# The end of a two-layer decoder on one core: the last two groups' steps written out, gathers issued first, and a routing count moved ahead

## The chip, the cores and the metric

The kernel runs on one core of a Trainium2 chip. The metric is the device time of one execution in microseconds, the median of several runs. TensorE (PE in the rows), VectorE (DVE), ScalarE (ACT) and GpSimd (POOL) each take their instructions in order from a queue of their own; SyncE (SP) issues transfers. They wait for each other through semaphores.

## What is computed

Eight sequences of 256 rows of 256 numbers pass through two decoder layers, all in float32. Layer 0 is causal self attention with 16 heads, cross attention to 120 context rows, and a mixture of eight experts of which each row takes two. Layer 1 is a gated self attention with an MLP, a cross attention with four heads and a mix of each row with the row before it. After each of the six parts the input is added and the row normalised:

```python
def _L1_xattn_ref(query_data, key_data, value_data, Wq, Wk, Wv, Wp, bp):
    q = split_heads(query_data, Wq); k = split_heads(key_data, Wk); v = split_heads(value_data, Wv)
    scores = jnp.einsum('bhqd,bhkd->bhqk', q, k) / np.sqrt(DK) + causal
    return jnp.einsum('bhqk,bhkd->bhqd', softmax(scores), v).transpose(0, 2, 1, 3).reshape(B, S, D_MODEL) @ Wp.T + bp

def _L1_ffn_ref(x, W_r, W_k, W_v, mu_r, mu_k):
    x_prev = jnp.concatenate([jnp.zeros((B, 1, C)), x[:, :-1, :]], axis=1)
    xr, xk = mu_r * x + (1.0 - mu_r) * x_prev, mu_k * x + (1.0 - mu_k) * x_prev
    r = jax.nn.sigmoid(xr @ W_r.T)
    return r * (jnp.square(jax.nn.relu(xk @ W_k.T)) @ W_v.T)

x = _layernorm(x + _L0_attn_ref(x, ...));  x = _layernorm(x + _L0_xattn_ref(x, ctx, ...))
x = _layernorm(x + _L0_ffn_ref(x, ...))
x = _layernorm(x + _L1_attn_ref(x, ...));  x = _layernorm(x + _L1_xattn_ref(x, ctx, ctx, ...))
x = _layernorm(x + _L1_ffn_ref(x, ...))
```

Inside `_L1_attn_ref` the attention's output is added to the row, normalised, and goes through the MLP: up to 1024 numbers, GELU, down to 256.

## The kernel before, in words

Three stages follow each other: `attention_layers`, `expert_layer` and `last_layers`. The 2048 rows are in four groups of two sequences, so a group is 512 rows or four tiles of 128. Nothing is scheduled by a tool: each stage has a block of instructions per engine, written in the order in which the engine runs them, and every wait is a `wait_ge` on a semaphore. An instruction behind a wait waits too, whatever it needs itself. The PSUM memory into which PE writes is eight banks; a product that reuses a bank waits until its reader is done.

**attention_layers.** At its end the routing of rows to experts is made up. DVE chooses two experts for each row (`choose`, its last lines L614 to L620), PE counts them (`count`, L461 to L465), and from the counts DVE works out each row's place (`rank`, from L628). One-hot tables in four batches of eight (made by POOL at L312 and L314, the last batch's second half by DVE at L759) are multiplied on PE (`place`, L473) into a table of sources. In PE's order for the last group all eight products of the third batch stand ahead of `count`. POOL and DVE both raise the semaphore `hothigh`.

**expert_layer.** Rows are handled in 39 tiles of 128, sorted by expert. For tile j POOL gathers the rows with an indirect DMA (`gather`, L810), PE turns them (`turn_rows`, L832), ACT copies them (L880), PE multiplies with the up weights (`up`, L846), ACT has copied the expert's up weights to a fixed place for that (`copy_weights`, L895) and takes the sigmoid (L884), POOL multiplies gate and sigmoid (L819), DVE finishes the hidden rows (L935 to L944), PE multiplies down (L857), DVE adds the bias (`result`, L951) and ACT issues the store (L910). ACT's order for a tile is: wait for the result of tile j, store it, copy the weights of tile j + 2, sigmoid of tile j + 1, copy the rows of tile j + 2. PE's order is: up of j + 1, turn j + 2, down of j. POOL issues the gather of tile j + 2 after the multiplication for tile j. SP has loaded three experts (1.5 MB each, with a bias) ahead of the stage and loads the next when one is found ready (`load_expert`, L156 to L160); at the start of the stage it issues the next three at once.

**last_layers.** The groups go through a pipeline of three steps: `a`, the self attention; `r`, its output product (`wout`), the MLP up (L1194 through `up`, eight products of 512 columns) and down (L1314, four tiles), then the context keys and values; `z`, the cross attention and the mix. A period works on `a` of one group, `r` of the one before and `z` of the one before that. Of the six periods (`PERIODS = G + 2`) the last two have no `a`: period 4 has `r` of group 3 (the last) and `z` of group 2, period 5 has only `z` of group 3. They run the same loop body with the parts for `a` left out.

The parts of `z` on which the change bears, in their order: queries (`wxq`), scores of the first sequence (`context_scores`, L1273), DVE's maximum (`context_max`, L1844 to L1849), 16 exponentials and sums on ACT (`context_exp`, L1556), DVE's scaling (`context_scale`, L1858), turning of the probabilities (`context_turn`, L1283) through one bank and ACT's copy (L1563), the same for the second sequence, sums (`context_sums`, L1294) and ACT's copies (L1607), the output product (`context_product`), the normalisation (L1796 to L1806 and L1790 on DVE, `rstd` on POOL), turning (L1203), ACT's copy (L1724), POOL's difference with the row before (L1172), DVE's mix (`mix`, L1814), products with `wk2` and `wr`, ACT's relu and tanh (L1733, L1736), DVE's square (L1987), and for each of four tiles a product with `wv2` and DVE's `mix_result` (L1898, L1900) through one bank.

## Time and profile before

| | |
|---|---|
| median of 3 runs | 1390.38 us (1387.86 to 1391.41) |
| the profiled execution's own time | 1385.69 us |
| its span | 1384.0 us |
| PE, DVE, ACT, POOL busy | 1141.3, 737.2, 575.2, 415.1 us |
| mean granted clock of TensorE | 0.934 |

The profiled execution's time is the span with 1.7 us around it. PE is busy for most of the span; its matrix instructions are pipelined and their ends modelled, so that busy is not the same as at full speed. The granted clock is 1.00 or 0.50: 2.4 or 1.2 GHz. `attention_layers` ends near 525 us, `expert_layer` near 776 us, and periods 4 and 5 of `last_layers` take the stretch from 1229.8 us on. A row of a timeline begins with its start and duration in microseconds; in brackets stands how long its engine had been idle and what ended that. One float32 product of two matrices (a `product` of `KD` = 2 parts) shows as four MATMUL records.

### The profile page before, as it was taken

Reading aid. Unit: us, or ns where it says so; the run is one execution under the profiler, and the core shown is the slowest. Engines: PE = TensorE matmul, PEld = TensorE weight load, DVE = VectorE, ACT = ScalarE, POOL = GpSimd, SP = SyncE. Lnnn points to the kernel's source line nnn. Section 1 sums busy time; section 2 is a strip of 40 time slices with the busy share of each in tenths; the row PEclk is TensorE's granted clock in tenths of the full one; section 3 lists DMA queues with packets and bytes.
Section 4 is the critical chain, followed back from the end, with each engine's and each line's share of the span. In section 5 each row is a group of like instructions: output and inputs, shape, how many; then the busy total and the mean of one; then the engine's idle time right before and its main releaser. Section 6 shows DMA issues by size and latency. Waiting matters only on the chain. (4 is left out here: it accounts for less than half of the span.)

```text
span 1384.0 us, 19896 instructions
## 1 busy us (share of the span) xinstructions
PE 1141.3 (82%) x6666; PEld 784.5 (57%) x6666; DVE 737.2 (53%) x2208; ACT 575.2 (42%) x1386; POOL 415.1 (30%) x508
## 2 busy tenths in 40 slices
PE   7889979988997865999999363877988998997965
PEld 3456456445645654988989332544645654664643
DVE  1563484367248443555555337484495868563334
ACT  1461272246117212444444052544665465434241
POOL 0250052025005673444444424033224222220111
PEclk9999999999999977999999776998999998997967
DMA  5000100020010407111111331001001000000000
GB/s 181 16 2 0 52 16 1 8 60 2 1 52 1 150 16 266 40 47 47 42 44 47 108 129 31 1 0 32 8 1 31 1 23 0 1 24 0 1 16 15
DMA packets 40223, 52.34 MB, mean 38 GB/s; under 512 B 10780, under 2 KB 33372, under 8 KB 40124
## 3 DMA queue, kind: packets, MB, share of 16 engines
q1 hardware_dynamic: 31100, 36.66, 8.2%
q0 software_dynamic: 3408, 9.31, 2.3%
q10 hardware_dynamic: 5616, 5.11, 1.1%
q8 instruction: 54, 0.88, 0.3%
q14 instruction: 45, 0.37, 0.1%
HBM read 41.76 MB, written 9.31 MB: 37 GB/s over the span
## 5 line engine op out<-in xcount | busy, mean ns | idle before, releaser
L1194 PE MATMUL bank<-words 128*128 128x512 f32 (+3 forms) x736 | 266.1, 512 | 36.3 <-ACT words L1547 17.3
L1194 PEld LDWEIGHTS bank<-words 128*128 128x128 f32 (+1 forms) x736 | 140.8, 199 | 137.4 <-issue 77.2
L357 PE MATMUL bank<-words 128*128 128x512 f32 x384 | 172.5, 601 | 8.3 <-DMA words<-in_wq 8.3
L323 POOL TENSOR_TENSOR words<-words 128x256 f32<-128x256 f32 (+1 forms) x128 | 103.5, 829 | 189.9 <-DVE words L694 189.9
L846 PEld LDWEIGHTS bank<-words 128*128 128x128 f32 x1248 | 146.9, 194 | 5.6 <-ACT words L880 3.7
L846 PE MATMUL bank<-words 128*128 128x128 f32 x1248 | 147.4, 277 | 3.1 <-ACT words L880 3.1
L565 ACT ACTIVATE words<-words 128x128 f32<-128x128 f32 (+1 forms) x256 | 113.3, 444 | 50.0 <-DVE words L689 50.0
L895 ACT ACTIVATE words<-words 128x2048 f32 x39 | 74.5, 1911 | 133.5 <-issue 133.5
L357 PEld LDWEIGHTS bank<-words 128*128 128x128 f32 x384 | 72.5, 193 | 90.1 <-issue 89.5
L547 ACT ACTIVATE words<-bank 128x512 f32<-128x512 f32 x48 | 28.7, 597 | 192.0 <-PE bank L357 192.0
L819 POOL TENSOR_TENSOR words<-words 128x512 f32<-128x512 f32 x39 | 49.4, 1268 | 136.3 <-ACT words L884 136.3
L604 DVE COPY words<-bank 128x512 f32<-128x512 f32 x48 | 33.2, 691 | 105.7 <-PE bank L357 105.4
L685 DVE CUSTOM_DVE_ANT_0 words<-bank,words 128x128 f32<-128x128 f32 (+1 forms) x256 | 76.0, 353 | 20.6 <-PE bank L368 18.7
L857 PE MATMUL bank<-words 128*128 x312 | 75.5, 385 | 0.7 <-DVE words L944 0.7
L128 POOL TENSOR_TENSOR words<-words 128x4 f32<-128x4 f32 x12 | 2.4, 200 | 243.5 <-DVE words L110 167.3
L1135 POOL TENSOR_TENSOR words<-words 128x2 f32<-128x2 f32 x32 | 6.9, 216 | 216.1 <-DVE words L1806 216.0
L935 DVE TENSOR_SCALAR words<-bank,words 128x128 f32<-128x128 f32 x156 | 44.1, 345 | 51.3 <-PE bank L846 51.1
L381 PE MATMUL bank<-words 128*128 128x128 f32 x384 | 55.1, 280 | 18.6 <-DVE words L700 10.5
L368 PE MATMUL bank<-words 64*128 64x128 f32 (+1 forms) x512 | 58.2, 348 | 8.6 <-DVE words L689 5.2
L394 PE MATMUL bank<-words 128*64 128x256 f32 (+1 forms) x512 | 55.8, 337 | 10.4 <-ACT words L573 9.4
L700 DVE COPY words<-bank 128x768 f32<-128x768 f32 x64 | 59.7, 932 | 8.3 <-PE bank L381 8.3
L381 PEld LDWEIGHTS bank<-words 128*128 128x128 f32 x384 | 41.0, 141 | 39.5 <-issue 31.8
(233 smaller groups left out, 2021.3 us busy)
## 6 DMA issues: line engine op xcount, KB each, us to landing
words<-in_w SPq DMA_DIRECT2D x8, 1024.0 KB, 10.3
y_slots<-words ACTq DMA_DIRECT2D x39, 128.0 KB, 1.7
words<-in_w SPq DMA_DIRECT2D x8, 512.0 KB, 10.9
words<-in_xt SPq DMA_DIRECT2D x4, 512.0 KB, 3.8
words<-in_x SPq DMA_DIRECT2D x4, 512.0 KB, 4.3
x_rows<-words SPq DMA_DIRECT2D x16, 128.0 KB, 1.8
words<-in_wm SPq DMA_DIRECT2D x2, 1024.0 KB, 6.8
out_x<-words SPq DMA_DIRECT2D x16, 128.0 KB, 1.8
```

The costliest lines, as they stand in the source:

```text
L323: last = pool.tensor_tensor(part, part, inv[:, j % SLOTS0, :, t:t + 1].to_broadcast([P, 2, P * (t + 1)]), ALU.mult)
L357: last = pe.matmul(bank[c % 2][:, :], w, r, start=k == 0, stop=k == KD - 1)
L368: last = pe.matmul(bank[SCORES[i % 2][n]][:, t * P:t * P + P * (t + 1)],  kt[r, m, b * S + t * P:b * S + (t + 1) * P], qt[r, m, b * S:b * ...
L381: last = pe.transpose(bank[2 + n][:, k * P:(k + 1) * P], prob[:, j % SLOTS0, n, c:c + P], ident[:, :])
L394: last = pe.matmul(bank[4 + j % 2][DH0 * n:DH0 * n + DH0, queries], v[:, 2 * b + k, h * DH0:(h + 1) * DH0], probt[:, j % 2, n, probs_of], ...
L565: last = act.activation(prob[:, i % SLOTS0, n, c], prob[:, i % SLOTS0, n, c], ACT.Exp, bias=negmax[:, i % SLOTS0, n, t:t + 1], scale=DH0 * ...
L685: dve.tensor_tensor_reduce(out=prob[:, i % SLOTS0, n, c], in0=bank[SCORES[i % 2][n]][:, c], in1=mask0[:, c], scale=1.0, scalar=-3e38, op0= ...
L700: dve.tensor_copy(probt[:, j % 2, :, :], turned).then_inc(tcopied, 1)
L846: last = pe.matmul(bank[(BANKG, BANKV)[half][j % 2]][:, c * P:(c + 1) * P], wfix[:, j % 2, k * 2 * FF + half * FF + c * P:k * 2 * FF + hal ...
L857: last = pe.matmul(bank[BANKY[j % 2]][:, 0:D], hidden[:, j % 2, k * P:(k + 1) * P], w2[:, bass.ds(e * W2 + k * D, D)], start=k == 0, stop= ...
L895: act.activation(wfix[:, j % 2, :], w1[:, bass.ds(e * W1, W1)], ACT.Copy).then_inc(wcopied, 1)
L1194: last = pe.matmul(out, w, r, start=i == 0, stop=i == len(pairs) - 1)
```

## The change

It has three parts. In `attention_layers` PE makes four of the eight products of the third one-hot batch ahead of `count` and four behind it; DVE's half of the last batch raises a semaphore of its own. In `expert_layer` POOL issues the gather of tile j + 2 ahead of the multiplication for tile j, and SP waits for the first two gathers before it loads the fourth expert. In `last_layers` periods 4 and 5 are no longer run by the loop (`PERIODS = G`); their instructions are written out on each engine. Products and elementwise work are the same in number of rows and columns; what differs is their order, the banks and how they are cut.

```diff
-            def place(first):
-                for n in range(first, first + OH):
+            def place(first, number=OH):
+                for n in range(first, first + number):
                     pe.wait_ge(hotlow, n + 1)
...
                         tail_gate(g)
                         if g == G - 1:
-                            place(2 * OH)
+                            place(2 * OH, OH // 2)
                     if c == COUNT:
                         count(g)
+                        if g == G - 1:
+                            place(2 * OH + OH // 2, OH // 2)
...
                 sp.sem_inc(ready, 1)
+                if e == 0:
+                    sp.wait_ge(gathered[0], 16)
+                    sp.wait_ge(gathered[1], 16)
                 if e + EARLY < NE:
                     load_expert(sp, dram, keep, e + EARLY)
...
             for j in range(SLOT_TILES):
-                pool.wait_ge(gated, j + 1)
-                pool.tensor_tensor(sig[:, :], gate[:, :], sig[:, :], ALU.mult).then_inc(mixed, 1)
                 if j + 2 < SLOT_TILES:
                     pool.wait_ge(rturned, j + 1)
                     gather(j + 2)
+                pool.wait_ge(gated, j + 1)
+                pool.tensor_tensor(sig[:, :], gate[:, :], sig[:, :], ALU.mult).then_inc(mixed, 1)
...
-        PERIODS = G + 2
+        PERIODS, LAST, OTHER = G, G - 1, G - 2
...
+            def last_up(b, i):
+                if b == 1:
+                    pe.wait_ge(m1gelu, i + 1)
+                for c in (2 * i, 2 * i + 1):
+                    last = product(bank[M1BANK[i]][:, batch(c % 2)], [(wm1[:, k, tok(c)], h5t[:, k, batch(b)]) for k in range(KD)])
+                last.then_inc(m1pair, 1)
...
+            context_scores(OTHER, 0)
+            turn(LAST, n5, 0, lambda t: h5[:, t, :], bank[2])
+            pe.wait_ge(n5.copied, 2 * LAST + 1)
+            last_up(0, 0)
+            last_up(0, 1)
+            context_scores(OTHER, 1)
...
+            for c in range(KD):
+                product(bank[2 * c][:, :], [(wk2[:, k, tok(c)], xk[:, k, :]) for k in range(KD)]).then_inc(kmm, 1)
...
+            context_scores(LAST, 0)
+            last_down(3)
...
+            last_queries(1, 1)
...
+            context_scores(LAST, 1, (4, 5))
+            context_turn(LAST, 0, (1, 3), lastsm)
...
+            last_turn(n7, 0, bank[0])
+            last_turn(n7, 1, bank[2])
+            last_mix(0, 6, 7, 1)
+            last_mix(1, 4, 5, 3)
+            last_values(0, 1)
+            last_values(1, 3)
...
+            context_exp(OTHER, 0)
+            mlp_rows(LAST, 0)
+            mlp_rows(LAST, 1)
+            context_exp(OTHER, 1)
+            act.preload_act_table_set("gelu_and_others")
...
+            act.preload_act_table_set("natural_log_exp_and_others")
+            context_exp(LAST, 0, sm=lastsm)
...
+            context_exp(LAST, 1, (4, 5), lastsm)
+            act.preload_act_table_set("gelu_and_others")
+            sums_copy(LAST, 0)
```

How the instructions stand, at the three places of which the prediction speaks. `bank` is the PSUM memory and `words` the SBUF, of which all tiles are parts; a line number is that of the kernel the rows are from.

PE at the end of `attention_layers`, before: the gate (L451), the one-hot products (L473), the count (L461 to L465), the source table (L534).

```order
L451 MATMUL bank<-words 128x8 x8
L473 MATMUL bank<-words 128x128 x8
L461 MATMUL bank<-words 128x32
L462 MATMUL bank<-words 128x32
L465 MATMUL bank<-words 128x8
L473 MATMUL bank<-words 128x128 x8
L534 MATMUL bank<-words 128x39
```

The same place now (products L477, count L462 to L466):

```order
L452 MATMUL bank<-words 128x8 x8
L477 MATMUL bank<-words 128x128 x4
L462 MATMUL bank<-words 128x32
L463 MATMUL bank<-words 128x32
L466 MATMUL bank<-words 128x8
L477 MATMUL bank<-words 128x128 x12
L540 MATMUL bank<-words 128x39
```

Four of the products that stood ahead of the count stand behind it.

PE in period 4 before, from the first scores of group 2 (L1273): turning of group 3's rows (L1203), the second scores, all turning of probabilities (L1283), the sums (L1294) with two up products of 512 columns between.

```order
L1273 MATMUL bank<-words 128x120 x8
L1203 MATMUL bank<-words 128x128 x8
L1273 MATMUL bank<-words 128x120 x8
L1283 MATMUL bank<-words 120x128 x16
L1294 MATMUL bank<-words 64x128 x4
L1194 MATMUL bank<-words 128x512 x2
L1294 MATMUL bank<-words 64x128 x4
L1194 MATMUL bank<-words 128x512 x2
L1294 MATMUL bank<-words 64x128 x8
```

Now (scores L1335, turning of rows L1265, of probabilities L1345, sums L1356, products L1256):

```order
L1335 MATMUL bank<-words 128x120 x8
L1265 MATMUL bank<-words 128x128 x4
L1256 MATMUL bank<-words 128x256 x8
L1335 MATMUL bank<-words 128x120 x8
L1265 MATMUL bank<-words 128x128 x4
L1256 MATMUL bank<-words 128x256 x8
L1345 MATMUL bank<-words 120x128 x8
L1256 MATMUL bank<-words 128x256 x8
L1345 MATMUL bank<-words 120x128 x8
L1256 MATMUL bank<-words 128x256 x8
L1356 MATMUL bank<-words 64x128 x16
```

The whole MLP up, in four pieces of eight matrix multiplications with 256 columns, now stands between the steps of group 2's cross attention.

PE in period 5 before, where group 3 is alone:

```order
L1203 MATMUL bank<-words 128x128 x8
L1194 MATMUL bank<-words 128x512 x4
L1273 MATMUL bank<-words 128x120 x16
L1283 MATMUL bank<-words 120x128 x16
L1294 MATMUL bank<-words 64x128 x16
L1194 MATMUL bank<-words 128x256 x8
L1203 MATMUL bank<-words 128x128 x8
L1194 MATMUL bank<-words 128x512 x4
L1194 MATMUL bank<-words 128x256 x16
```

And now, from the products that precede group 3's first scores:

```order
L1256 MATMUL bank<-words 128x512 x4
L1335 MATMUL bank<-words 128x120 x8
L1256 MATMUL bank<-words 128x256 x16
L1265 MATMUL bank<-words 128x128 x4
L1256 MATMUL bank<-words 128x256 x12
L1335 MATMUL bank<-words 128x120 x8
L1345 MATMUL bank<-words 120x128 x8
L1356 MATMUL bank<-words 64x128 x8
L1345 MATMUL bank<-words 120x128 x8
L1256 MATMUL bank<-words 128x256 x4
L1356 MATMUL bank<-words 64x128 x8
L1256 MATMUL bank<-words 128x256 x4
```

Between group 3's two scores now stand 28 matrix multiplications of 256 columns: the last down tile, group 2's products with `wr` and `wv2`, and group 3's second queries. Behind this the probabilities of the first sequence are turned and summed before those of the second are turned.

## Rows read from the trace of the kernel before

**Rows 1.** Timeline of PE at the end of the routing.
```profile
507.87 2.59 PE L473 MATMUL bank<-words 128*128 128x128 f32 x10
...
514.44 0.47 PE L461 MATMUL bank<-words 128*128 128x32 f32 x2
...
515.15 0.57 PE L465 MATMUL bank<-words 128*128 128x8 f32 x2
```
**Rows 2.** Timeline of DVE at the same place.
```profile
510.55 0.89 DVE L620 TENSOR_TENSOR words<-words 128x8 f32<-128x8 f32 x4
...
515.76 0.28 DVE L628 TENSOR_TENSOR words<-words,bank 128x32 f32<-128x32 f32 x2 [3.65 <-PE bank L465]
```
**Rows 3.** Entry into the experts: first gather, and PE's waits for gathered rows.
```profile
525.87 1.22 POOL L810 DMA_INDIRECT words<-x_rows,words  x1 [3.43 <-POOLq L165]
...
534.27 0.69 PE L832 MATMUL bank<-words 128*128 128x128 f32 x2 [9.66 <-DMA words<-x_rows,words]
...
549.32 0.44 PE L832 MATMUL bank<-words 128*128 128x128 f32 x2 [1.80 <-DMA words<-x_rows,words]
```
**Rows 4.** POOL's instructions between 660 and 700 us, gathers among them.
```profile
DMA to landing us min/median/max: 3.5/3.6/4.1
```
**Rows 5.** POOL's multiplication for the third and the last tile.
```profile
555.80 1.26 POOL L819 TENSOR_TENSOR words<-words 128x512 f32<-128x512 f32 x1 [5.17 <-ACT words L884]
...
771.58 1.26 POOL L819 TENSOR_TENSOR words<-words 128x512 f32<-128x512 f32 x1 [4.89 <-ACT words L884]
```
**Rows 6.** Waits of PE between 560 and 772 us: total, times, longest.
```profile
PE bank L832 <- DMA words<-x_rows,words: 8.3, 19, 1.0
```
**Rows 7.** Timeline of ACT and POOL in one expert tile.
```profile
650.17 1.91 ACT L895 ACTIVATE words<-words 128x2048 f32 x1 [3.21 <-issue]
...
652.68 1.27 POOL L819 TENSOR_TENSOR words<-words 128x512 f32<-128x512 f32 x1 [3.31 <-ACT words L884]
```
**Rows 8.** Windows of PE in periods 4 and 5: us, busy, clock, DMA.
```profile
1245.30:1265.80 20.50, 11.31 (x48) 0.50 0.00 1
...
1327.20:1351.10 23.90, 14.29 (x74) 0.50 0.00 1
...
1358.00:1364.80 6.80, 4.23 (x5) 0.50 0.00 0
...
1229.80:1384.00 154.20, 109.40 (x482) 0.82 0.04 12
```
**Rows 9.** Waits of PE in period 5, from 1317.7 us.
```profile
PE bank L1273 <- ACT words L1556: 5.2, 1, 5.2
PE bank L1194 <- DVE words L1814: 4.1, 1, 4.1
PE bank L1283 <- DVE words L1858: 3.8, 1, 3.8
PE bank L1203 <- DVE words L1790: 2.3, 2, 1.7
PE bank L1194 <- DVE words L1898: 1.6, 3, 0.6
```
**Rows 10.** Period 4: PE's second turning, ACT's copy of group 3's rows, PE's second scores.
```profile
1247.04 1.12 PE L1203 MATMUL bank<-words 128*128 128x128 f32 x4 [2.43 <-DVE words L1790]
...
1249.40 1.97 ACT L1532 ACTIVATE words<-bank,words 128x256 f32<-128x256 f32 x4
...
1249.60 2.07 PE L1273 MATMUL bank<-words 64*128 64x120 f32 x16 [1.44 <-ACT words L1556]
```
**Rows 11.** ACT's change of table in period 4, and the first GELUs.
```profile
1270.41 1.28 ACT L1717 ACT_TABLE_LOAD   x1
1271.70 1.27 ACT L1547 ACTIVATE words<-bank,words 128x512 f32<-128x512 f32 x2
```
**Rows 12.** PE: five products in a stream, and one alone between waits.
```profile
1312.80 4.49 PE L1194 MATMUL bank<-words 128*128 128x256 f32 x20 [0.51 <-DVE words L1898]
...
1372.06 1.13 PE L1194 MATMUL bank<-words 128*128 128x256 f32 x4 [0.59 <-DVE words L1898]
```

More of the change, by code:

```diff
@@ L1474, in _ @@
                     pe.wait_ge(rsig, NT * z + NT)
[L1476 to L1487 removed]
+                if r is None:
                     pe.wait_ge(qkt, NT * a + NT)
@@ L1514, in _, with last_down @@
                     context_values(r)
+            def last_up(b, i):
[4 more added lines that the diff above has]
+                last.then_inc(m1pair, 1)
+            def last_down(t):
+                if t >= 2:
+                    pe.wait_ge(n6.added, NT * LAST + t - 1)
+                product(bank[(3, 1)[t % 2]][:, 0:D], [(m1t[:, k, tok(t)], wm2[:, k, :]) for k in range(MC)]).then_inc(n6.product, 1)
@@ new lines, in last_values @@
+            def last_values(b, out):
+                pe.wait_ge(lastkact, b + 1)
+                for i in range(HALF):
+                    last = product(both(out, b)[:, i, :], [(lastrl[:, k, tok(HALF * b + i)], wv2[:, k, :]) for k in range(KD)])
+                last.then_inc(lastv, 1)
+            pe.wait_ge(utc, QUADS1 * G)
+            turn_heads(LAST, 0)
+            turn_heads(LAST, 1)
+            pe.wait_ge(xvr, GB * OTHER + GB)
+            for b in range(2):
+                turn(OTHER, n6, b, lambda t: x(OTHER, t), bank[6 + b])
@@ new lines, in _ @@
+            turn_output(LAST, 0)
+            turn_heads(LAST, 2)
+            turn_heads(LAST, 3)
+            turn_output(LAST, 1)
+            pe.wait_ge(n6.copied, 2 * OTHER + 2)
+            for c in range(KD):
+                product(bank[6 + c][:, :], [(wxq[:, k, tok(c)], x4t[:, k, :]) for k in range(KD)]).then_inc(xq, 1)
+            for t in range(NT):
+                pe.wait_ge(ogc, 2 * LAST + t // HALF + 1)
+                if t >= 2:
+                    pe.wait_ge(n5.added, NT * LAST + t - 1)
+                else:
+                    pe.wait_ge(ogr, NT * LAST + NT)
+                product(bank[t % 2][:, 0:D], [(ogt[:, k, tok(t)], wout[:, k, :]) for k in range(KD)]).then_inc(n5.product, 1)
@@ new lines, in _ @@
+            context_scores(LAST, 0)
+            last_down(3)
+            pe.wait_ge(mixed, 2 * OTHER + 2)
+            for b in range(2):
+                for i in range(HALF):
+                    last = product(both(4 + b, b)[:, i, :], [(xr[:, k, tok(HALF * b + i)], wr[:, k, :]) for k in range(KD)])
+                last.then_inc(rmm, 1)
+            last_turn(n6, 1, bank[3])
+            pe.wait_ge(kact, KD * OTHER + KD)
+            for t in range(NT):
+                if t >= 2:
+                    pe.wait_ge(n8.added, NT * OTHER + t - 1)
+                product(bank[2 * (t % 2)][:, 0:D], [(rl[:, k, tok(t)], wv2[:, k, :]) for k in range(KD)]).then_inc(n8.product, 1)
@@ L1764, in _, with last_gelu, last_rows @@
                         values_copy(r, b)
+            def last_gelu(b, i):
+                act.wait_ge(m1pair, MC // 2 * b + i + 1)
+                for c in (2 * i, 2 * i + 1):
+                    last = act.activation(m1t[:, c, batch(b)], bank[M1BANK[i]][:, batch(c % 2)], ACT.Gelu, bias=bm1[:, c:c + 1])
+                last.then_inc(m1gelu, 1)
+            def last_rows(b, source):
+                act.wait_ge(n6.turned, 2 * LAST + b + 1)
+                act.activation(half(x4t, b), turned_rows(bank[source]), ACT.Copy).then_inc(n6.copied, 1)
@@ new lines, in _ @@
+            for b in range(2):
+                act.wait_ge(n6.turned, 2 * OTHER + b + 1)
+                act.activation(half(x4t, b), turned_rows(bank[6 + b]), ACT.Copy).then_inc(n6.copied, 1)
+            output_copy(LAST, 0)
+            output_copy(LAST, 1)
+            for c in range(KD):
+                act.wait_ge(xq, KD * OTHER + c + 1)
+                act.activation(qxt[:, c, :], bank[6 + c][:, :], ACT.Copy).then_inc(xqr, 1)
+            context_exp(OTHER, 0)
+            mlp_rows(LAST, 0)
@@ new lines, in _ @@
+            last_queries_copy(0, 5)
+            act.wait_ge(mixed, 2 * OTHER + 2)
+            for c in range(KD):
+                act.wait_ge(kmm, KD * OTHER + c + 1)
+                act.activation(rl[:, c, :], bank[2 * c][:, :], ACT.Relu).then_inc(relu, 1)
+            for b in range(2):
+                act.wait_ge(rmm, NT * OTHER + b + 1)
+                act.activation(rs[:, rows_of(b), :], both(4 + b, b), ACT.Tanh, scale=0.5).then_inc(rsig, 1)
+            act.preload_act_table_set("natural_log_exp_and_others")
@@ new lines, in _ @@
+            mix(OTHER, MUR, xr)
+            add_product(LAST, n6, 2, bank[3])
+            for c in range(KD):
+                dve.wait_ge(relu, KD * OTHER + c + 1)
+                dve.tensor_tensor(rl[:, c, :], bank[2 * c][:, :], rl[:, c, :], ALU.mult).then_inc(kact, 1)
+            add_product(LAST, n6, 3, bank[1])
+            context_max(LAST, 0)
+            normalise(LAST, n6, lambda t: x(LAST, t), 1)
+            dve.wait_ge(rsig, NT * OTHER + 2)
+            for t in range(NT):
+                dve.wait_ge(n8.product, NT * OTHER + t + 1)
+                dve.scalar_tensor_tensor(rs[:, t, :], rs[:, t, :], 1.0, bank[2 * (t % 2)][:, 0:D], ALU.add, ALU.mult).then_inc(n8.added, 1)
+                dve.drain()
+                dve.scalar_tensor_tensor(x(OTHER, t), rs[:, t, :], 0.5, x(OTHER, t), ALU.mult, ALU.add)
```

309 lines of the change are left out of this document (260 added, 49 removed).

## The prediction, made before the changed kernel had run

> **What bounds the kernel now.** I read the page, then the timelines of PE at three places, the waits of PE there, and its windows with the granted clock. PE is busy for 82% of the span (the table above), and where it is not, it stands behind short chains of the other engines. So the edits are worth what they take out of those chains. Three places count.
>
> At the end of the routing PE makes one-hot products until it may count. DVE had chosen the experts at 510.55 + 0.89 = 511.44 us, the count began at 514.44 and ended at 515.72, and DVE went on at 515.76 after 3.65 us of idling for it [rows 1, 2].
>
> At the entry into the experts the first gather is issued at 525.87 and its rows are there at 534.27: 8.4 us, in which PE does nothing [rows 3]. Later gathers take 3.5 to 4.1 us, 3.6 in the middle [rows 4]. The first shares the DMA engines with the three experts of 1.5 MB that SP issues in the same microsecond.
>
> In periods 4 and 5 PE is busy for 109.4 of 154.2 us, at a mean clock of 0.82 [rows 8]. 11.31 + 14.29 + 4.23 = 29.8 us of that is at 1.2 GHz, which at 2.4 GHz would be 14.9. So the stretch is 94.5 us of work at full clock, 14.9 us that the low clock adds, and 44.8 us without work, of which the last 7.4 are DVE's, POOL's and the store's after PE's last product.
>
> **The change part by part.**
>
> *Count moved ahead.* Four products stand ahead of it instead of eight. Five of them took 2.59 us from 507.87 [rows 1], so four end near 509.95, before DVE has chosen at 511.44. The count takes the same 515.72 − 514.44 = 1.28 us and ends at 512.75, and DVE goes on some 2.9 us earlier. What comes behind (DVE's ranks and half one-hot tables, POOL's other half) waits for these ranks and moves with them; POOL is done with its earlier tables before that. The four products behind the count are hidden by DVE's ranking. **2.9 us.** The separate semaphore costs nothing: its only waiter is the same PE product.
>
> *SP waits for the first two gathers.* Gather 0 then runs alone and should land 3.6 us after its issue, at 529.5 instead of 534.27: **4.8 us**. Between 4.1 and 3.5 us of landing it is 4.3 to 4.9; below, nothing, if the 8.4 us is the price of a first gather and not of the sharing. What SP issued at 525.2 it now issues near 531, some 6 us later; the fourth expert is needed after three experts' tiles, at six microseconds a tile, far behind. The Trainium skill, "DMA: Bandwidth & Descriptors", section on queues, rings and completion order, speaks against so much: each DMA engine goes round between the queues that have work, packet by packet. By that rule an estimate would be that sharing at most doubles the 3.6 us, and the wait is worth 3.6 instead of 4.8 us.
>
> *Gathers issued one multiplication earlier.* POOL's own order costs nothing: the issue (some 1.4 us) falls into the 3.3 us in which POOL waits for ACT [rows 7], and starts when it did before. But it is for a tile one later, so each gather has a tile's time more. Three things follow. The third tile's gather no longer stands behind the first multiplication, is issued near 530, and the 1.80 us at 549.32 goes [rows 3]; DVE's result, waiting behind it, comes 2.0 us earlier: **2.0**. In the steady part PE waits 8.3 us for gathers, 19 times [rows 6], but most of this is not on the path: 36 multiplications take 771.58 − 555.80 = 215.8 us, 5.99 each [rows 5], and the loop that sets them is ACT's: copy of weights 1.91, sigmoid 0.6, POOL 1.27 [rows 7], DVE's two instructions 1.1, store and the register read before the next copy 1.0. That is 5.9 us and holds no gather. Its steps stand at 6.03 us for the first 16 tiles and at 5.88 for the later ones, and only single steps exceed these, by 1.5 us together: **1.5**. The last tile has no weights to copy and PE's wait of 1.0 us counts in full: **1.0**. For this part the ends are 0 and 8.3 + 2.0; I stay near the sum 4.5.
>
> *Periods 4 and 5.* The work is the same 94.5 us: a half of 256 columns costs half of 512. What changes is how much stands idle, how often the pipe runs empty, and the clock.
> Idle in period 5 [rows 9]: the 5.2 us for ACT's exponentials goes, because group 2's products with `wr` and `wv2` and group 3's last down tile lie there now. The 1.6 us of the four separate `wv2` results, and the 0.6 before them, go, since they are two products for a half each in banks of their own. The 4.1 and 2.3 us around normalisation and mix (6.4) shrink to about 3.7: one half's chain is covered by the other's products. The 3.8 us for the second scaling stays. Two banks instead of one for turned probabilities take 1.3 of 2.2 us of copies. Sum 11.1 us.
> Idle in period 4: the up products fill the 3.8 us and 2.2 us of the same chain only in part, since each half waits for a GELU or a copy; I count 0.2 saved. One wait is added: the first up product needs ACT's copy of its rows, which stands behind 16 exponentials. The copies begin at 1249.40, half of 1.97 us later PE may start, 1250.4, where the first half's rows are turned at 1247.04 − 2.43 = 1244.6. In place of 2.43 + 1.44 = 3.9 us of waits [rows 10] this is some 5.5: 1.6 lost. Down and `wv2` of different groups no longer follow one another tile by tile, 1.8 saved. Sum 0.4.
> Each wait also lets the pipe run empty: a product alone is 1.13 us, in a stream 4.49 / 5 = 0.90 [rows 12]. Some 15 waits go: 15 × 0.23 = 3.5.
> Clock: it fell at 1245.3 and 1327.2 among waits and came back after steady work. With up products between the scores I expect about 11 us of addition instead of 14.9, as one of the two long stretches stays (the last group's probabilities and scaling). 3.9, with ends of 0 and 10.
> After PE's last product the same chain remains: 0.
> Sum 11.1 + 0.4 + 3.5 + 3.9 = 18.9; laid out with every wait on all four queues at the durations of the trace, 19 to 25 come out, by where the clock falls. I take **20**. The ends are 11 (idle time alone) and 27.
> What ACT's tables cost: the new order has three changes where there were four, but one now lies right before group 3's first exponentials and one behind its second. Load and first GELU follow each other, 1.28 and then 1271.70 [rows 11]; group 2's products cover that. "ScalarE: Activation LUTs", section "What ACT_TABLE_LOAD costs", in the Trainium skill gives about 1.4 us of drain on top; the rows show none. By the page the gain of 20 would be some 2.8 less.
>
> The sum is 2.9 + 4.8 + 4.5 + 20 = 32.2 us. Against the profiled execution's own 1385.69 us this gives 1353.5; that execution was 4.7 us below the median of 1390.38, so on the median's scale it is **1358 us**. A difference of over 0.3%, 4 us, is what a measurement of this kernel can tell.
>
> **The rivals.**
>
> *Half chains bring idle time only.* The clock stays as poor as before, since the interleaved pieces are short and each waits for GELU or copy, and the pipe runs empty as often. Then the end gives 11 to 12: 1390.4 − 2.9 − 9.3 − 11.5 = 1367. For it: the rows at low clock hold work in pieces of one or two microseconds [rows 8]. Against: the new pieces are 3.6 us.
>
> *The first gather is slow by itself.* Nothing is shared away, the 4.8 us stays where it is and with it perhaps half of what follows: 1358 + 4.8 + 2 = 1365. For it: it is the first indirect transfer of the stage. Against: the third, issued under the same loads, was late too.
>
> *The end gains more.* With few waits left the clock stays high through the older group's cross attention: 27 instead of 20, 1351.
>
> *Slower: the clock stays low through periods 4 and 5.* If the cut into halves and the many orders between queues leave PE with a short wait in every piece, so that it is granted 1.2 GHz from 1245 on, all work behind that, some 80 us at full clock, is doubled, and the low clock adds 80 us where the forecast has 11: 1358 + 69 = 1427. It decides for slower from 11 + 32 = 43 us of work at the low clock. The Trainium skill, "TensorE: Matmul & The Clock Gate", has the throttled clock as the default that only activity lifts, which is this mechanism. Against: between 1265.8 and 1327.2 PE kept 2.4 GHz with a dozen short waits.
>
> *The change does not do what it says* hardly applies: its order is to be seen on the queues.
>
> **How the numbers follow.** The forecast has 0.60, the gain at the end without the clock 0.14, the slow first gather 0.10, the better clock 0.12, the slower case 0.03; 0.01 is left for no change. The forecast's own range is 1352 to 1364; with the neighbours and 3 us for where the clock happens to fall in the unchanged middle it is 1348 to 1368. Faster 0.95, same 0.02, slower 0.03.
>
> **What would show it.** Right: DVE's L628 successor starts near 512.9; PE's first turned rows near 526.6 (2.9 earlier and 4.8 less); no PE wait for gathered rows in the steady part and steps of 6.03 and 5.88 us on POOL; between the first `turn_heads` of group 3 and the last normalisation about 132 us instead of 152; PE's wait before the first up product about 5.5 us. Wrong: gathers that still take over 6 us at the entry, tile steps under 5.8 us (then the gather was on the path and the gain is larger), over 20 us of PE work at clock 0.5 in the last 130 us, or a time above 1368.

## The result, and the profile after

The changed kernel takes 1355.14 us (median of 4 runs, 1354.0 to 1355.9) where the kernel before, run beside it, takes 1389.22 us. The ratio is 0.9753, with an interval of 0.9736 to 0.9769. The forecast was 1358 us and faster.

The profiled execution took 1355.9 us, with a span of 1354.0 us. PE is busy for 1137.6 us of it (1141.3 before), at a mean clock of 0.942 (0.934). The two profiled spans differ by 1384.0 − 1354.0 = 30.0 us, the medians by 34.1.

**The count.** Timelines of PE and of DVE at the end of the routing, which answer to [rows 1, 2] (start, duration, engine, line and operation; in brackets the idle time ahead and what ended it):

```profile
507.90 2.05 PE L477 MATMUL bank<-words 128*128 128x128 f32 x8
511.73 0.63 PE L462 MATMUL bank<-words 128*128 128x32 f32 x2 [1.77 <-DVE words L626]
...
512.60 0.57 PE L466 MATMUL bank<-words 128*128 128x8 f32 x2
513.02 2.05 PE L477 MATMUL bank<-words 128*128 128x128 f32 x8
```

```profile
508.08 0.19 DVE L739 COPY words<-bank 128x32 f32<-128x32 f32 x1 [3.89 <-PE bank L452]
...
513.21 0.28 DVE L634 TENSOR_TENSOR words<-words,bank 128x32 f32<-128x32 f32 x2 [0.87 <-PE bank L466]
```

Four products end at 509.95 us, before DVE has chosen, and PE now waits for DVE (1.77 us). DVE's own wait for the count shrinks from 3.65 to 0.87 us, and it goes on at 513.21 instead of 515.76.

**The experts.** POOL's first gathers and the multiplications for the third and the last tile, and PE's first turning of gathered rows; they answer to [rows 3, 5]:

```profile
523.33 1.22 POOL L819 DMA_INDIRECT words<-x_rows,words  x1 [3.43 <-POOLq L165]
...
546.18 1.27 POOL L831 TENSOR_TENSOR words<-words 128x512 f32<-128x512 f32 x1 [3.20 <-ACT words L893]
...
759.32 1.27 POOL L831 TENSOR_TENSOR words<-words 128x512 f32<-128x512 f32 x1 [3.16 <-ACT words L893]
```

```profile
526.46 0.69 PE L841 MATMUL bank<-words 128*128 128x128 f32 x2 [4.39 <-DMA words<-x_rows,words]
```

The rows of the first gather are used 526.46 − 523.33 = 3.13 us after its issue (8.40 before). PE's waits between 550 and 765 us, which answer to [rows 6] (total, times, longest):

```profile
PE bank L855 <- ACT words L889: 4.2, 16, 0.5
PE bank L866 <- DVE words L953: 0.8, 1, 0.8
```

No wait for gathered rows is left, and PE waits for ACT instead. POOL's steps stand at 6.03 and then 5.88 us as before, so the gathers did not set them. That ACT's loop does fits the sum of its durations; no run here changes that loop, so it is not shown. The last step is 759.32 − 754.89 = 4.43 us.

**The end.** Windows of PE in the changed kernel, from the first turning of heads of group 3 on, the stretches at low clock first; they answer to [rows 8] (length; busy time and records; clock; DMA share; GB/s):

```profile
1235.60:1245.90 10.30, 5.18 (x12) 0.50 0.00 0
1256.20:1262.90 6.70, 5.54 (x13) 0.50 0.00 0
1321.00:1324.40 3.40, 3.05 (x12) 0.51 0.00 0
1334.70:1338.10 3.40, 3.40 (x9) 0.52 0.02 5
1220.04:1354.00 133.96, 101.33 (x529) 0.90 0.05 14
```

And its waits there, which answer to [rows 9]:

```profile
PE bank L1256 <- ACT words L1739: 5.9, 1, 5.9
PE bank L1265 <- DVE words L2089: 5.6, 4, 3.2
PE bank L1345 <- DVE words L2157: 3.8, 1, 3.8
PE bank L1345 <- ACT words L1770: 3.5, 2, 2.7
PE bank L1256 <- ACT words L1977: 1.5, 1, 1.5
```

The stretch is 133.96 us instead of 154.14 (1229.86 to the end): 12.2 us less without work (32.6 instead of 44.8) and 8.0 us less of busy time. At low clock lie 5.18 + 5.54 + 3.05 + 3.40 = 17.2 us, which add about 8.6 us (half of it) where it was 14.9. The exponentials' 5.2 us, the waits for single `wv2` results and most of the wait for the mix are gone. The largest wait is now the one that the change added, 5.9 us for ACT's copy of rows; the forecast had 5.5.

### The profile page after: what moved, and what is told of

The parts are those of the page before. It is cut to its first block and busy times, and to the rows that moved or that the text cites. A ratio compares the mean times of both kernels' runs of the same rounds, so it can differ in the third digit from the quotient of the medians.

```text
span 1354.0 us, 20004 instructions
## 1 busy us (share of the span) xinstructions
PE 1137.6 (84%) x6714; PEld 788.5 (58%) x6714; DVE 735.5 (54%) x2208; ACT 574.0 (42%) x1389; POOL 415.8 (31%) x509
## 5 line engine op out<-in xcount | busy, mean ns | idle before, releaser
L1256 PE MATMUL bank<-words 128*128 128x256 f32 (+3 forms) x848 | 282.9, 487 | 37.2 <-ACT words L1754 19.0
L1256 PEld LDWEIGHTS bank<-words 128*128 128x128 f32 (+1 forms) x848 | 165.6, 202 | 130.5 <-issue 70.0
L855 PE MATMUL bank<-words 128*128 128x128 f32 x1248 | 151.7, 281 | 8.4 <-ACT words L889 6.7
L691 DVE CUSTOM_DVE_ANT_0 words<-bank,words 128x128 f32<-128x128 f32 (+1 forms) x256 | 76.0, 353 | 20.6 <-PE bank L369 18.4
L382 PE MATMUL bank<-words 128*128 128x128 f32 x384 | 55.9, 282 | 17.0 <-DVE words L706 9.1
L953 DVE SCALAR_TENSOR_TENSOR words<-words 128x512 f32<-128x512 f32 x39 | 27.0, 694 | 67.3 <-POOL words L831 67.2
```

Source lines behind the costliest of these rows:

```text
L382: last = pe.transpose(bank[2 + n][:, k * P:(k + 1) * P], prob[:, j % SLOTS0, n, c:c + P], ident[:, :])
L691: dve.tensor_tensor_reduce(out=prob[:, i % SLOTS0, n, c], in0=bank[SCORES[i % 2][n]][:, c], in1=mask0[:, c], scale=1.0, scalar=-3e38, op0= ...
L855: last = pe.matmul(bank[(BANKG, BANKV)[half][j % 2]][:, c * P:(c + 1) * P], wfix[:, j % 2, k * 2 * FF + half * FF + c * P:k * 2 * FF + hal ...
L1256: last = pe.matmul(out, w, r, start=i == 0, stop=i == len(pairs) - 1)
```

## The parts one by one

The medians of the kernel before scatter by 12 us on one chip (1382.04 to 1394.34 in 29 runs), and parts of 3 to 5 us drown in that. So I cut each profiled execution at four events that the timelines show: the issue of the first gather, PE's first turning of gathered rows, the end of the last expert product, and the first turning of heads of group 3. In microseconds, each number being the difference of two times of the rows:

| kernel | gather, issue to use | then to the end of the experts | then to the last group's heads | then to the end |
|---|---|---|---|---|
| before | 8.40 | 241.45 | 454.14 | 154.14 |
| changed | 3.13 | 237.00 | 456.58 | 133.96 |
| e1_count | 8.03 | 241.50 | 461.39 | 153.92 |
| e2_loads | 3.10 | 245.32 | 455.99 | 153.89 |
| e3_gather | 8.62 | 236.86 | 456.00 | 153.77 |
| e4_end | 8.27 | 241.16 | 455.36 | 133.55 |
| u1_scores_behind | 2.88 | 238.55 | 456.04 | 137.93 |
| s1_rows | 2.98 | 236.98 | 456.25 | 129.99 |
| s2_warm | 3.03 | 238.57 | 455.16 | 133.94 |
| s3_warm_late | 3.08 | 236.98 | 453.52 | 134.27 |
| s4_warm_start | 3.07 | 236.97 | 453.38 | 133.82 |
| s5_rows_warm | 3.11 | 237.00 | 452.71 | 121.19 |

Where nothing was edited, a stretch repeats within half a microsecond at the end, and twice the experts took 1.6 us more. Between experts and the last heads, which nobody touched but s4 and s5, it varies by 8 us: 453.52 (s3_warm_late) to 461.39 (e1_count). There PE's busy time varies with it, 350.67 us before and 358.38 in e1_count, at mean clocks of 0.90 and 0.87, while the time without work stays at 103.5 and 103.0 us. So in these traces most of the scatter lies there. The time ahead of the first gather is in no column: its issue stands at 525.87 to 528.36 us in the four kernels without the count's edit and at 523.20 to 525.06 in the eight with it.

**The count alone.** In the kernel before:

```diff
-                            place(2 * OH)
+                            place(2 * OH, OH // 2)
...
                         count(g)
+                        if g == G - 1:
+                            place(2 * OH + OH // 2, OH // 2)
```

> The kernel before with the count moved ahead alone. My theory: DVE goes on 2.6 to 2.9 us earlier (the first L634 of the last group near 513.0 us instead of 515.76), everything behind shifts by that, and the time falls by 2.6 us. Rival (the four products behind the count delay the table of sources): PE's source table starts less than 1 us earlier and the time stays within 1 us.

DVE goes from its copy of the gate's result to the first rank in 513.56 − 508.38 = 5.18 us, where the kernel before took 515.76 − 508.06 = 7.70: 2.5 us. The rival spoke of the table of sources (L534 before, L540 here), which the four products might hold up:

```profile
521.75 0.65 PE L540 MATMUL bank<-words 128*128 128x39 f32 x2 [0.67 <-DVE words L769]
```

It begins 521.75 − 508.38 = 13.37 us after the same copy, where it was 523.96 − 508.06 = 15.90: again 2.5 us. The median fell from 1389.88 to 1387.09 us, ratio 0.9987 (0.997 to 1.0004), which alone would prove nothing. By the rows the rival falls.

**SP's wait alone.**

```diff
                 sp.sem_inc(ready, 1)
+                if e == 0:
+                    sp.wait_ge(gathered[0], 16)
+                    sp.wait_ge(gathered[1], 16)
```

> The kernel before with only SP's wait for the first two gathers. My theory (sharing with SP's loads made the first gather slow): issue to landing falls from 8.4 to 3.1 to 3.6 us, PE's wait for it falls by about 5 us, the wait of 1.8 us for the third tile's gather and those of the steady part stay, and the time falls by 5 us. Rival (a first gather is slow by itself): 8.4 us again, time unchanged.

The first gather takes 3.10 instead of 8.40 us, so it was the loads beside it and not the first gather itself. But the experts then take 3.9 us longer, and only 1.4 us of the 5.3 is kept. PE in e2_loads, third, fourth and fifth tile:

```profile
544.62 0.44 PE L835 MATMUL bank<-words 128*128 128x128 f32 x2 [1.92 <-DMA words<-x_rows,words]
...
550.96 0.44 PE L835 MATMUL bank<-words 128*128 128x128 f32 x2 [0.59 <-DMA words<-x_rows,words]
...
559.10 0.44 PE L835 MATMUL bank<-words 128*128 128x128 f32 x2 [2.41 <-DMA words<-x_rows,words]
559.38 3.32 PE L860 MATMUL bank<-words 128*128 x8
```

The loads that SP held back now run while tiles three to five are gathered: between 552 and 559 us the DMA engines are busy for 0.84 of the time, where it was 0.11. The wait of 2.41 us stands in no row of the kernel before, and after it the down product takes 3.32 us where others take 1.89 (the mean granted clock from 559.1 to 562.7 us is 0.59). POOL's step there is 567.06 − 557.43 = 9.63 us instead of 6.03. The median moved to 1386.21 us, ratio 0.9985 (0.9963 to 1.0006). My theory was right on the gather and wrong that the other waits would stay as they were.

**The gathers first, alone.**

```diff
             for j in range(SLOT_TILES):
-                pool.wait_ge(gated, j + 1)
-                pool.tensor_tensor(sig[:, :], gate[:, :], sig[:, :], ALU.mult).then_inc(mixed, 1)
                 if j + 2 < SLOT_TILES:
                     pool.wait_ge(rturned, j + 1)
                     gather(j + 2)
+                pool.wait_ge(gated, j + 1)
+                pool.tensor_tensor(sig[:, :], gate[:, :], sig[:, :], ALU.mult).then_inc(mixed, 1)
```

> The kernel before with only the gather issued ahead of the multiplication. My theory: the first gather still takes 8.4 us, the third tile's wait of 1.8 us goes, single long steps of the steady part go, steps stay at 6.03 and 5.88 us; time down by 4.5 us. Rival (the third gather was late because of the loads, not because of its place behind the multiplication): the first steps gain nothing and the time falls by 2.5 us or less.

The experts take 4.6 us less (236.86), the first gather 8.62. PE's waits between 560 and 772 us show the same two rows as in the changed kernel, and the third tile's wait is gone, with all loads running: the place behind the multiplication had made it late, and the rival falls. Median 1384.25 us, ratio 0.9965 (0.9948 to 0.9982).

The kernel before, e2_loads, e3_gather and the changed kernel make a square for the expert stage. Taken alone the two edits of the expert stage bring 1.4 and 4.4 us (sums of the first two columns against before: 249.85, then 248.42 and 245.48), together 249.85 − 240.13 = 9.7. The 3.9 us more are the collision, which gathers with a tile's time to spare can bear: in the changed kernel, in the 25 us from 531 us on, gathers land in 5.2 us in the median where the lone first one took 3.1, and nobody waits for them. These are the DMA issues of that stretch:

```profile
words<-in_w SPq DMA_DIRECT2D x3, 1024.0 KB, 12.1
...
words<-x_rows,words POOLq DMA_INDIRECT x4, 5.2
```

**The end alone.** The kernel before with `last_layers` of the changed one.

> The kernel before with only the end of the last stage written out. My theory: the stretch from the first turning of heads of the last group to the end is 134 us instead of 154 (12 us less idle time of PE, 7 to 8 us less at the low clock), everything ahead is as before, and the time falls by 20 us. Rival (part of the 20 us came from the earlier parts, by where the clock happens to fall): 15 us or less.

The last stretch is 133.55 us, 20.6 less than before, with PE busy for 100.85 us of it; the rest is as before. Median 1367.86 us, ratio 0.9857 (0.9831 to 0.9883). It takes nothing from the earlier parts. What each piece of this rewriting is worth is read from rows below; only two of its orders were tried by themselves.

## What the end is made of

**A fill undone.** I had said that the exponentials' 5.2 us go because other products lie there now. Here two of these blocks are put ahead of the scores again:

```diff
-            context_scores(LAST, 0)
             last_down(3)
             pe.wait_ge(mixed, 2 * OTHER + 2)
...
                 last.then_inc(rmm, 1)
+            context_scores(LAST, 0)
```

> The changed kernel with one fill undone: group 3's last down tile and group 2's products with wr (7.2 us of work) stand ahead of group 3's first scores, not between them and the turning that follows. Theory A (mine at the prediction: this fill takes the place of the wait of 5.2 us for the exponentials): some 5 us of waits come back, the last stretch is 139 us. Theory B (in the changed kernel ACT starts these exponentials only at 1307.31, behind the tanh and a table load that wait for the same products, 8 us after PE had written the scores; so the scores had 7 us to spare): exponentials start within 0.5 us of where they did, the turning of rows 2.5 us later, and the last stretch is 135.8 us.

The last stretch is 137.93 us: 4.0 more, between the two, and the rows show why. Here the exponentials start 86.88 us after the stretch's start, in the changed kernel 87.27: not later at all, as theory B had it. Another cause was not tried: the second scores now lie in banks 4 and 5 and no longer wait for the exponentials at all, where before they reused banks 6 and 7. In the changed kernel the exponentials end at 1310.16 us and the second scores begin at 1313.54, so either alone, the products between or the banks, would have done. PE in this kernel and in the changed one:

```profile
1305.10 1.16 PE L1335 MATMUL bank<-words 64*128 64x120 f32 x16
1308.88 1.11 PE L1265 MATMUL bank<-words 128*128 128x128 f32 x4 [2.63 <-DVE words L2089]
1309.79 7.92 PE L1256 MATMUL bank<-words 128*128 128x256 f32 x24
```

```profile
1297.10 1.16 PE L1335 MATMUL bank<-words 64*128 64x120 f32 x16
1298.18 7.17 PE L1256 MATMUL bank<-words 128*128 128x256 f32 x32
1305.68 0.76 PE L1265 MATMUL bank<-words 128*128 128x128 f32 x4 [0.32 <-DVE words L2089]
```

The turning of rows comes 1.6 us later (87.21 against 85.64 after the stretch's start), with a wait of 2.63 us ahead of it, in which the clock falls: the six products behind it take 7.92 us where four take 3.62 at 2.4 GHz. Idle time grew by 33.69 − 32.63 = 1.1 us only, busy time by 104.24 − 101.33 = 2.9, with the same work. So theory B was right on the chain but too low on the price (135.8 us), and three quarters of that are clock. The median is 1360.11 us, against 1355.14 of the changed kernel.

**The added wait taken out.** ACT stands idle until its exponentials begin, and could copy the rows in that time:

```diff
-            context_exp(OTHER, 0)
             mlp_rows(LAST, 0)
+            context_exp(OTHER, 0)
             mlp_rows(LAST, 1)
```

> The changed kernel, and ACT copies the first half of the last group's turned rows ahead of the 16 exponentials, not behind them. My theory (the wait of 5.9 us before the first up product is nothing but this place in ACT's queue, since ACT stands idle for 7.6 us ahead of the exponentials while the rows are turned): the wait falls to about 1 us, the 5.1 us of work behind it run at 2.4 GHz, and the stretch from the turning of heads to the end falls from 134.0 to about 127 us. Rival (ACT's chain of exponentials, table and copies bounds what follows): the wait only moves to the next scores and turnings, 131 us or more.

PE in the changed kernel, then in this one:

```profile
1234.03 0.76 PE L1265 MATMUL bank<-words 128*128 128x128 f32 x4 [0.83 <-DVE words L2089]
1240.71 6.23 PE L1256 MATMUL bank<-words 128*128 128x256 f32 x16 [5.92 <-ACT words L1739]
1246.87 1.16 PE L1335 MATMUL bank<-words 64*128 64x120 f32 x16
```

```profile
1233.41 0.76 PE L1265 MATMUL bank<-words 128*128 128x128 f32 x4 [0.83 <-DVE words L2089]
1235.28 5.12 PE L1256 MATMUL bank<-words 128*128 128x256 f32 x16 [1.11 <-ACT words L1739]
1240.33 1.16 PE L1335 MATMUL bank<-words 64*128 64x120 f32 x16
```

The wait falls to 1.11 us, as expected. The whole stretch is 129.99 us, between my 127 and the rival's 131. Idle time fell by 5.1 us (27.53), but PE's busy time rose by 1.1: the four low stretches hold 20.0 us of work here. Windows of s1_rows:

```profile
1234.80:1238.20 3.40, 2.92 (x7) 0.51 0.00 0
1248.40:1255.20 6.80, 5.01 (x13) 0.50 0.00 0
1313.30:1320.10 6.80, 5.63 (x20) 0.50 0.00 0
1326.90:1333.70 6.80, 6.42 (x17) 0.50 0.01 2
```

The later waits of 2.7, 3.7 and 3.2 us are unchanged in length, so the rival's mechanism is not what happened; behind two of them the clock stays low for twice as long as in the changed kernel. The median is 1351.63 us (ratio to before 0.9738, 0.9709 to 0.9767).

**Work that nobody reads, in the waits.** These kernels compute additional products into a free bank; the output is unchanged. The first has one such block:

```diff
+            warm(20, bank[3])
             pe.wait_ge(n5.copied, 2 * LAST + 1)
             last_up(0, 0)
```

where `warm(n, out)` issues n matrix multiplications of 256 columns, which nobody waits for or reads.

> The changed kernel with 20 matrix multiplications of 256 columns, whose results nobody reads, in PE's wait of 5.9 us before the first up product. My theory (the clock falls because PE stands still, and the price is the work behind the wait): the wait is filled, the clock stays at 1.00 and the first four up products take 3.6 instead of 6.2 us, so the last stretch is 131.4 us instead of 134.0. Rival (the clock does not depend on this wait, or the added work delays the products behind it): 134 us or more.

```profile
1234.95 8.80 PE L1614 MATMUL bank<-words 128*128 128x256 f32 x40
1243.59 3.62 PE L1256 MATMUL bank<-words 128*128 128x256 f32 x16
```

The clock stays up and the four products take 3.62 us, not 6.23. But one float32 multiplication shows as two records of 0.22 us, as the front of this document says of a product, and I had taken it for one: the block lasts 8.80 us, and the products behind it start 23.23 us after the stretch's start where they started at 20.67: 2.6 us later, which is what was won. That is the second half of the rival. The stretch is 133.94 us. The same mistake is in the next one, in the later waits (here PE's wait for the second copy of rows stands ahead of the second turning):

> The changed kernel with unread matrix multiplications in the three later waits (10 and 6 around the second turning of group 2's probabilities, 15 before the last group's third turning, 13 before its last turning of rows). My theory: three low stretches of some 3.4 us with about 10 us of work in all go, the last stretch is 129 us instead of 134.0. Rival (these waits lie on ACT's and DVE's chain, which sets the time whatever the clock of PE): less than 2 us gained.

From 1244 to 1343 us PE keeps 1.00 here, and the blocks are each too long (20 and 12 records for waits of 2.7 and 1.5 us, 30 for 3.8, 26 for 3.2). The stretch is 134.27 us, which is the rival's number and not my 129; but with the blocks too long it does not tell the two apart. The fourth stands at the start of the stage:

```diff
             pe.wait_ge(const, 1)
+            pe.wait_ge(n3.stats, 1)
+            for _ in range(10):
+                pe.matmul(bank[7][:, 0:256], wgate[:, 0, tok(0)], wgate[:, 0, 0:256], start=True, stop=True)
             turn_front(0)
```

> The changed kernel with 10 unread matrix multiplications at the start of the last stage, issued 4 us before the first turned rows, where PE has stood idle for 27 us and then works for 20 us at 1.2 GHz. My theory: the clock rises about 4 us after their start, the first forms' 11.3 us become 6 to 8 us, and the stretch from the last expert product to the turning of the last group's heads is about 4 us shorter than 456.6. Rival (what follows waits for ACT and DVE anyway, so a faster PE waits longer): less than 1 us; the stretch has varied between 454.1 and 461.4 us in kernels that share it.

The block takes 7.31 us, the first rows are turned 2.8 us later than in the changed kernel, the forms behind them take 8.86 instead of 11.29 us, and DVE's scan begins 42.9 us after the experts' end where it was 43.0: nothing won. The 3.2 us by which the third column is shorter lie within its scatter (s3_warm_late has 453.52 without this edit).

**Both, with the right lengths.**

```diff
+            pe.wait_ge(backed[2 * NT - 1], 16)
+            for _ in range(9):
+                pe.matmul(bank[7][:, 0:256], wgate[:, 0, tok(0)], wgate[:, 0, 0:256], start=True, stop=True)
             turn_front(0)
...
+            warm(2, bank[3])
             pe.wait_ge(n5.copied, 2 * LAST + 1)
...
             context_turn(OTHER, 0)
-            context_turn(OTHER, 1)
             pe.wait_ge(n5.copied, 2 * LAST + 2)
+            warm(5, bank[3])
+            context_turn(OTHER, 1)
+            warm(3, bank[3])
...
             context_sums(LAST, 1, (6, 7), lastpxt)
+            warm(8, bank[1])
             context_turn(LAST, 2, (1, 3), lastsm)
...
             last_turn(n7, 0, bank[0])
+            warm(6, bank[1])
             last_turn(n7, 1, bank[2])
```

with s1_rows' order on ACT.

> The changed kernel with the first rows' copy ahead of the exponentials, and unread multiplications in half the numbers of the earlier tries (a matrix multiplication shows as two records of 0.22 us, and I had sized them by one): 2 before the first up product, 5 and 3 around group 2's second turning, 8 and 6 in the last group's waits, and 9 at the start of the stage, from the last gathered rows on (near 782 us) in place of the mean's (788 us). My theory (the price of a wait is its length and the work behind it at half clock): against the kernel with the copy ahead alone, 130.0 us, the last stretch loses 1.5 + 2.0 + 1.8 + 2.7 us of low clock and is 122 to 123 us; the start gains 2 us. Rival (the clock is won back but the products wait for ACT and DVE instead): 127 us or more.

Windows of PE in this kernel, from the heads to PE's last product and to the end, and two of the waits as they now stand:

```profile
1216.21:1329.64 113.43, 103.64 (x577) 1.00 0.04 12
...
1216.21:1337.40 121.19, 103.64 (x577) 0.98 0.05 16
```

```profile
1303.96 3.72 PE L1617 MATMUL bank<-words 128*128 128x256 f32 x16
1307.79 1.09 PE L1345 MATMUL bank<-words 128*120 128x128 f32 x8
...
1314.43 2.75 PE L1617 MATMUL bank<-words 128*128 128x256 f32 x12
1317.84 0.76 PE L1265 MATMUL bank<-words 128*128 128x128 f32 x4 [0.65 <-DVE words L2102]
```

The last stretch is 121.19 us, somewhat under the 122 to 123 expected: 8.8 less than in s1_rows, against the 8.0 that I had added up. The rival had 127 or more and falls. All of PE's work in it runs at 2.4 GHz. Of the 103.64 us that it is busy, 1.03 + 2.32 + 1.46 + 3.72 + 2.75 = 11.3 are unread, so 92.4 are work: in the changed kernel 101.33 − 8.6 = 92.7, in the kernel before 109.34 − 14.9 = 94.4. DVE's scan at the start of the stage begins 803.60 − 763.50 = 40.1 us after the experts, 2.9 earlier; in the third column this is lost in the scatter (452.71 against 453.52 at the least without it). The median is **1340.62 us** (6 runs, 1339.24 to 1347.15), ratio to the kernel before 0.967 (0.9643 to 0.9696): below that of the changed kernel, whose interval ends at 0.9736. The medians lie 14.5 us apart; in the profiled executions the last stretch accounts for 133.96 − 121.19 = 12.8.

## Why the prediction was right, step by step

The sum was 32.2 us: 2.9 + 4.8 + 4.5 + 20. On the profiled pair it came out as 2.5 + 5.3 + 4.5 + 20.2 = 32.5, less 2.4 us that the untouched middle took longer in that execution: 30.0, with rounding. The medians show 34.1, since the profiled execution of before lay 3.5 us below its median, for which the forecast allowed 4.7, and that of the changed kernel 0.8 above its own. For the end the terms added up to 18.9, and I took 20 from a layout on all queues; in the 11.1 for period 5 there is a slip too, as the terms named give 11.4. Measured are 20.2.

- **Count, 2.9.** Measured 2.5 to 2.6. DVE's choice ended 0.2 us later than in the rows of before, and the count took 513.17 − 511.73 = 1.44 us, not the 1.28 of a count that follows products directly.
- **First gather, 4.8.** Measured 5.3: alone it takes 3.1 us, less than the 3.5 to 4.1 of the steady part. The rival that a first gather is slow by itself falls with e2_loads. "DMA: Bandwidth & Descriptors" of the Trainium skill, in its section on queues, rings and completion order, says that engines go round between queues packet by packet, from which I had estimated a gain of 3.6 us; the measurement decides, 8.4 is 2.7 times 3.1. The three loads were not issued in one microsecond, as I wrote: the rows have them from 525.20 to 530.77 us, while the gather was under way. What I did not see is that the loads would collide with the next gathers. I wrote that the fourth expert is needed far behind, and asked only who waits for the loads, not who runs beside them. It cost nothing here because the other edit was there: alone, e2_loads gave 3.9 of its 5.3 us back.
- **Gathers first, 4.5.** Measured 241.45 − 237.00 = 4.5 in the pair and 4.6 alone. The third tile's step fell by 8.02 − 6.05 = 1.97 us (2.0 forecast). The steps of 6.03 and 5.88 us stayed, so the steady gathers were no bound, though PE waited 8.3 us for them. The last step gave 6.16 − 4.43 = 1.7 us, where I had 1.0 from PE's wait, and the rest, 0.8 us, is less than the 1.5 for the other long steps. That the sum came out to a tenth is partly luck.
- **Idle time at the end, 11.5.** Measured 12.2. Of the waits that I named, those for exponentials and `wv2` results are gone, 3.8 us for the second scaling stayed, normalisation and mix kept 3.2 + 0.4 us (3.7 forecast), and the added one was 5.9. I had put that one at 5.5, but my own two times, 1250.4 and 1244.6, are 5.8 apart. That the exponentials' wait goes because products fill it is one of two reasons that would each do, as the banks changed too.
- **Pipe refill, 3.5, and clock, 3.9.** Their sum of 7.4 is 8.0 in the rows, but the shares were wrong. The clock gave about 6.3 (14.9 to 8.6), and full-clock work fell by 1.7 us only (94.4 to 92.7). PE's waits in the stretch went from 32 to 18, so the number of waits was right and the price was not: 0.23 us each came from one product alone against one in a stream, and 1.7 / 14 = 0.12 is left. It was luck that the errors cancelled. "Half chains bring idle only" falls by the same numbers.
- **The end gains more**, 27 us by a clock that stays high, did not come: PE fell to 1.2 GHz at 1235.6 and at 1256.2 us. s5_rows_warm shows that there was more to have: 154.14 − 121.19 = 33.0 us.
- **The slower case**, the clock low from 1245 on, did not come: 17.2 us of work at low clock, and 43 would have decided. "TensorE: Matmul & The Clock Gate" of the Trainium skill, section "What's actually happening", with the low clock as the default that activity lifts, agrees with s5_rows_warm, where against s1_rows only activity was added in the last stretch, and PE kept 1.00 to its last product.
- **Tables of ACT.** All three loads at the end are followed at once, for instance 1253.19 + 1.28 = 1254.47 us and the next instruction at 1254.48. The 1.4 us of drain that "ScalarE: Activation LUTs" of the Trainium skill, section "What ACT_TABLE_LOAD costs", gives is in none of these rows.

ACT in the changed kernel, the load and the copy behind it:

```profile
1253.19 1.28 ACT L2016 ACT_TABLE_LOAD   x1
1254.48 0.60 ACT L1770 ACTIVATE words<-bank 120x512 f32<-120x512 f32 x1
```

What stays open: why the untouched middle runs at a lower clock in some executions than in others, and whether its own long waits (19.3 us at one place) would repay the same filling, which I did not try. Not tried either were the second scores in the old banks, and the changed kernel without SP's wait.

## What to carry to other kernels

A transfer that is held back to let another pass does not vanish: look at what runs when it is let go, and give that work slack first, as the pair of edits here did. Price a wait of PE at its length plus half of the low-clock work behind it, and read both from windows; here the second part was as large as the first in places, and unread products a little shorter than the wait took it away (3.72 us in a wait of 3.75), while blocks one and a half times to nearly twice as long gave it all back. Where parts are smaller than the scatter of the whole, compare stretches between events, not medians.

## What was not expected of the hardware

- A shorter wait did not mean less work at low clock. With the first wait cut from 5.92 to 1.11 us, 20.0 us of work lay at 1.2 GHz instead of 17.2, behind later waits of unchanged length (3.24 us, then 6.42 us of work at the low clock in place of 3.40).
- Gathers of the same size took 3.1 us alone and 8.0 to 8.6 us beside three expert loads whose issue began 0.7 us earlier (525.20 against 525.87 us in the kernel before), but beside loads already under way 5.2 us in the median in the changed kernel and 6.5 in e2_loads.
- With PE at 2.4 GHz throughout, its work of periods 4 and 5 comes to 92.4 us in a stretch of 121.19 us; the kernel before lost 14.9 us of its 154.14 to the clock alone.
